# Expert stage of an audio tower: first weights stationary, bias folded into the gelu, token ids routed before the scores

## The reference

```python
h = tok(x)                                    # 16 x 255 tokens, 256 wide
h = h + attn(layernorm(h))                    # gated scan over the tokens, 8 heads
x = layernorm(h)                              # (16*255, 256)
logits = x @ w_red @ normalised(wg).T         # 8 experts
gates = softmax(logits); scores = max(gates); idx = argmax(gates)
g = gelu(x @ W1[idx] + b1[idx])               # 256 -> 512, exact gelu
o = (g @ W2[idx] + b2[idx]) * scores          # 512 -> 256
return h + o
```

## Time and profile before

| | us |
|---|---|
| median of 3 runs | 554.67 (554.56 to 558.87) |
| the profiled execution itself | 554.61 |
| its span in the trace | 552.9 |
| PE busy | 511.7 (93% of the span) |
| DVE, ACT, POOL busy | 454.5, 231.4, 193.1 |
| expert stage, first up product to last result | 412.8 to 543.0 |

### The profile page before, as it was taken

The page is one execution under the profiler, slowest core; times in us unless marked ns, Lnnn a source line. Parts: engine busy times, 40 slices in busy tenths (PEclk is TensorE's granted clock), DMA queues, the critical chain, the costliest instruction groups (busy, mean ns, idle before and its releaser), DMA issues. The chain is left out here.

```text
span 552.9 us, 12548 instructions
## 1 busy us (share of the span) xinstructions
PE 511.7 (93%) x3439; PEld 368.3 (67%) x3439; DVE 454.5 (82%) x1180; ACT 231.4 (42%) x447; POOL 193.1 (35%) x283
## 2 busy tenths in 40 slices
PE   5998999999999999999988879999868999999992
PEld 4875667766677766777654657777436777777771
DVE  2878888988889888888898899999858888888881
ACT  0436354664545554545635421222105444444440
POOL 5553323312232213222121212222142656665642
PEclk9999999999999999999998998999989999999997
DMA  5711212122122121221123033443521222222320
GB/s 126 249 40 38 76 40 76 43 71 76 38 76 67 47 76 47 67 76 38 38 54 97 24 99 98 114 107 92 209 96 41 85 73 86 74 81 79 78 56 1
DMA packets 34937, 42.14 MB, mean 76 GB/s; under 512 B 8454, under 2 KB 26103, under 8 KB 34644
## 3 DMA queue, kind: packets, MB, share of 16 engines
q1 hardware_dynamic: 25508, 27.59, 16.5%
q0 software_dynamic: 3744, 9.34, 5.8%
q10 hardware_dynamic: 5648, 4.75, 2.8%
HBM read 32.97 MB, written 9.59 MB: 77 GB/s over the span
## 5 line engine op out<-in xcount | busy, mean ns | idle before, releaser
L533 PE MATMUL banks<-proj,xnT_h 128*128 128x512 f16 x384 | 115.1, 382 | 4.3 <-DVE early L1231 4.2
L514 PE MATMUL banks<-early 128*128 128x256 f16 x768 | 86.8, 273 | 1.1 <-DVE early L1206 1.1
L514 PEld LDWEIGHTS banks<-early 128*128 128x128 f16 x768 | 75.1, 98 | 9.7 <-DVE early L1206 1.4
L533 PE MATMUL banks<-proj,xnT_l 128*128 128x512 f16 x192 | 73.1, 381 | 0.0
L533 PEld LDWEIGHTS banks<-proj,xnT_h 128*128 128x128 f16 x384 | 37.5, 98 | 41.2 <-DVE early L1231 4.9
L1855 POOL DMA_INDIRECT vo<-token_rows,vo x39 | 40.1, 1028 | 54.8 <-DVE proj L1689 35.3
L767 PE MATMUL banks<-w2h,vo 128*128 x312 | 57.5, 273 | 0.2 <-DVE vo L1664 0.2
L748 PE MATMUL banks<-w1h,vo 128*128 x156 | 52.9, 380 | 2.8 <-DVE vo L1657 2.8
L1003 ACT ACTIVATE vo<-banks 128x256 f16<-128x256 f32 x39 | 14.9, 383 | 81.0 <-PE banks L735 81.0
L1793 POOL TENSOR_TENSOR w1l<-stage,w1h 128x512 f32 (+1 forms) x16 | 19.0, 1186 | 84.0 <-ACT w1h L887 84.0
L1860 POOL DMA_INDIRECT out<-proj,vo x39 | 39.8, 1020 | 18.8 <-issue 10.8
(11 more groups left out here) (259 smaller groups left out, 1256.5 us busy)
## 6 DMA issues: line engine op xcount, KB each, us to landing
early<-in_x SPq DMA_DIRECT2D x16, 512.0 KB, 3.3
stage<-in_W SPq DMA_DIRECT2D x32, 256.0 KB, 2.8
early<-lam_by_chunk SPq DMA_DIRECT2D x32, 68.0 KB
token_rows<-rows ACTq DMA_DIRECT2D x16, 129.0 KB, 2.5
early<-lam_by_head SPq DMA_DIRECT2D x16, 128.0 KB, 3.0
rows<-in_b SPq DMA_DIRECT2D x1, 2048.0 KB, 7.1
token_rows<-rows ACTq DMA_DIRECT2D x16, 112.9 KB, 2.0
rows<-in_b SPq DMA_DIRECT2D x1, 1024.0 KB, 9.2
```

Of the source, the lines that this page charges most:

```text
L514: last = mm(bank(2 + j, D), x_[:, k, at:at + P], w[:, KG * half + k, :], start=(half == 0 and k == 0 and x_ is gT_h and w is wtok_h), stop ...
L533: last = mm(dst, a, c, start=(i == 0), stop=(i == n - 1))
```

## The change

What it does, part by part:

1. `up` swaps its operands: the weights are stationary and the rows stream. Per slot there are 4 (groups of 128 hidden units) x 2 x 3 = 24 matmuls of 128 columns where there were 6 of 512. The result has hidden units on the partitions, in two banks for each of two buffers, so it needs no turning: `transpose_gelu` is gone.
2. The bias of a unit is then one number per partition. ACT adds it inside the gelu, four ACTIVATEs of 128 columns per slot, with the bias's address from a register (ACT loads the expert number too). DVE's `add_bias` is gone. The bias table is a 16 KB load, turned once by PE; the 2 MB load is gone.
3. The split of the gelu reads SBUF; `down` runs one slot behind `up`, no longer two; `xh` and `xl` have two buffers.
4. The ids are found by their own product (32 matmuls of 39 columns), straight after the first `carried` table and `at_place`; the scores by a second one (32 of 78 columns) behind it. DVE makes `gather_id` ahead of the score halves, and the rest of the score work (`keep_scores`) after the first two slots' rows. POOL makes the arguments of the exponential.
5. `keep_busy(9)` after mixing tile 6, 30 for 28 in routing, 10 between the two find products, none behind them.

```diff
-            def up(i, e):
+            def up(i, v, e):
                 pe.wait_ge(s["xdl_done"], i + 1)
-                if i >= 1:
-                    pe.wait_ge(s["pre_done"], i)
-                for c in range(DC):
-                    for x_, w in ((xh, w1h), (xh, w1l), (xl, w1h)):
-                        last = mm(bank(0), x_[:, c, :], w[:, bass.ds(e * DC + c, 1), :].rearrange("p a b -> p (a b)"),
-                                  start=(c == 0 and w is w1h and x_ is xh), stop=(c == DC - 1 and x_ is xl))
-                last.then_inc(s["m1_ready"], 1)
-
-            def transpose_gelu(i, w):
-                pe.wait_ge(s["gelu_done"], i + 1)
                 if i >= 2:
-                    pe.wait_ge(s["g_done"], i - 1)
+                    pe.wait_ge(s["gelu_done"], FC * (i - 1))
                 for f in range(FC):
-                    last = tr(bank(4 + w)[:, f * P:f * P + P], gel[:, f * P:f * P + P], ident[:])
-                last.then_inc(s["gt_ready"], 1)
+                    for c in range(DC):
+                        for w, x_ in ((w1h, xh), (w1l, xh), (w1h, xl)):
+                            last = mm(banks[:, 4 * v + f // 2, f % 2 * P:f % 2 * P + P],
+                                      w[:, bass.ds(e * DC + c, 1), f * P:f * P + P].rearrange("p a b -> p (a b)"), x_[:, v, c, :],
+                                      start=(c == 0 and w is w1h and x_ is xh), stop=(c == DC - 1 and x_ is xl))
+                    if f % 2 == 1:
+                        last.then_inc(s["m1_ready"], 1)
...
             for i in range(SLOTS):
-                up(i, experts[i])
                 if i + 1 < SLOTS:
                     experts[i + 1] = expert_of(i + 1)
                     transpose_rows(i + 1)
+                up(i, i % 2, experts[i])
                 if i >= 1:
-                    transpose_gelu(i - 1, (i - 1) % 2)
-                if i >= 2:
-                    down(i - 2, i % 2, experts[i - 2])
...
+                    down(i - 1, (i - 1) % 2, experts[i - 1])
...
+            def gelu(i, w, e):
+                if i >= 2:
+                    act.wait_ge(s["g_done"], i - 1)
+                for f in range(FC):
+                    if f % 2 == 0:
+                        act.wait_ge(s["m1_ready"], 2 * i + f // 2 + 1)
+                    af(gel[:, w, f, :], banks[:, 4 * w + f // 2, f % 2 * P:f % 2 * P + P], ACT.Gelu,
+                       bias=b1_turned[:, bass.ds(e * FC + f, 1)]).then_inc(s["gelu_done"], 1)
...
+            pe.wait_ge(s["carried_ready"], 1)
+            find(found_ids, 0, 1).then_inc(s["found_ready"], 1)
+            keep_busy(10)
             pe.wait_ge(s["carried_ready"], 3)
...
+            find(banks[:, 7, 0:2 * SLOTS], 1, 2).then_inc(s["scores_found"], 1)
...
+                    if (p, k) == (1, 2):
+                        keep_busy(9)
```

More of the change, by code:

```diff
@@ L709, in _ @@
                 pair(p, ahead=p < PAIRS - 1)
+            pe.wait_ge(s["b1_in"], 16)
+            tr(bank(4, E * FC), b1_rows, ident[0:E * FC, 0:E * FC]).then_inc(s["b1_mm"], 1)
             keep_busy(14)
@@ L716, in _, with find @@
             mm(bank(0, 256), count_rows[:, 0, :], ohf, start=True, stop=True).then_inc(s["counts"], 1)
-            keep_busy(28)
-            pe.wait_ge(s["carried_ready"], 3)
[L721 to L728, removed]
+            keep_busy(30)
+            def find(dst, v, n):
+                for q in range(4):
+                    if n == 1:
+                        pe.wait_ge(s["places_ready"], q + 1)
+                    for t in range(8 * q, 8 * q + 8):
+                        last = mm(dst, at_place[:, t // 2, :, t % 2],
+                                  carried[:, t // 2, v:v + n, :, t % 2].rearrange("p v i -> p (v i)"),
+                                  start=(t == 0), stop=(t == TILES - 1))
+                return last
+            pe.wait_ge(s["carried_ready"], 1)
+            find(found_ids, 0, 1).then_inc(s["found_ready"], 1)
+            keep_busy(10)
+            pe.wait_ge(s["carried_ready"], 3)
+            find(banks[:, 7, 0:2 * SLOTS], 1, 2).then_inc(s["scores_found"], 1)
             def transpose_rows(i):
@@ L1603, in _ @@
                       slot_twice[:].unsqueeze(1).to_broadcast(TS), ALU.is_equal))
+            r.settle()
+            tt(carried[:, :, 0], in_slot, by_pairs(ids16[:]).unsqueeze(2).to_broadcast(TS),
+               ALU.mult).then_inc(s["carried_ready"], 1)
+            for q in range(4):
+                four = slice(4 * q, 4 * q + 4)
+                TP = [P, 4, P, 2]
+                tt(at_place[:, four], by_pairs(place_of)[:, four].unsqueeze(2).to_broadcast(TP),
+                   place_twice[:].unsqueeze(1).to_broadcast(TP), ALU.is_equal).then_inc(s["places_ready"], 1)
             dve.wait_ge(s["r_exp"], 1)
@@ L1611, in _ @@
             r.step(tt(score, score, valid[:], ALU.mult))
+            dve.wait_ge(s["found_ready"], 1)
+            ts(gather_id, found_ids, float(ID_MIDDLE), None, ALU.add).then_inc(s["route_ready"], 1)
             r.settle()
@@ L1619, in _ @@
                    ALU.mult).then_inc(s["carried_ready"], 1)
-            for q in range(4):
-                four = slice(4 * q, 4 * q + 4)
-                TP = [P, 4, P, 2]
-                tt(at_place[:, four], by_pairs(place_of)[:, four].unsqueeze(2).to_broadcast(TP),
-                   place_twice[:].unsqueeze(1).to_broadcast(TP), ALU.is_equal).then_inc(s["places_ready"], 1)
             S7 = [P, SLOTS, E - 1]
@@ L1631, in _, with keep_scores @@
             copy(sloti, slotf).then_inc(s["experts_ready"], 1)
-            dve.wait_ge(s["found_ready"], 1)
-            ts(gather_id, found[:, 0], float(ID_MIDDLE), None, ALU.add).then_inc(s["route_ready"], 1)
-            r.step(copy(score_high, found[:, 1]))
-            r.settle()
-            r.step(tt(slot_score, found[:, 2], score_high, ALU.add))
-            r.settle()
-            r.step(ts(empty, slot_score, 0.0, float(OUT_OF_RANGE + ID_MIDDLE), ALU.is_equal, ALU.mult))
-            r.step(ts(slot_id, found[:, 0], float(ID_MIDDLE), None, ALU.add))
-            r.settle()
-            r.end()
-            tt(store_id, slot_id, empty, ALU.add).then_inc(s["slot_ids_ready"], 1)
+            def keep_scores():
+                dve.wait_ge(s["scores_found"], 1)
+                r.step(copy(score_high, found_scores[:, 0]))
+                r.step(ts(slot_id, found_ids, float(ID_MIDDLE), None, ALU.add))
+                r.settle()
+                r.step(tt(slot_score, found_scores[:, 1], score_high, ALU.add))
+                r.settle()
+                r.step(ts(empty, slot_score, 0.0, float(OUT_OF_RANGE + ID_MIDDLE), ALU.is_equal, ALU.mult))
+                r.settle()
+                r.end()
+                tt(store_id, slot_id, empty, ALU.add).then_inc(s["slot_ids_ready"], 1)
             def norm_rows(i):
@@ L1850, in _ @@
                 root2(2 * h + 1)
+            T8 = [P, TILES, E]
+            pool.wait_ge(s["mx_done"], 1)
+            ptt(lg, rows[:, :, ROWC:ROWT], mx.unsqueeze(2).to_broadcast(T8), ALU.subtract).then_inc(s["lg_steps"], 1)
+            pool.wait_ge(s["rstd2_ready"], TILES)
+            pool.wait_ge(s["lg_steps"], 1)
+            ptt(lg, lg, rows[:, :, 1:2].to_broadcast(T8), ALU.mult).then_inc(s["r_args"], 1)
             def load(i):
```

116 lines of the change are left out of this document (52 added, 64 removed).

## The result

The changed kernel takes 581.06 us (median of 4 runs, 580.54 to 581.36) where the kernel before, run beside it, takes 555.12 (554.56 to 558.87). The ratio is 1.045, 95% interval 1.040 to 1.050: slower, by about 26 us. Its profiled execution took 580.99 us; the span is 579.2.

What follows compares the result with a forecast made beforehand. The prediction took the array to bound the kernel before (3.26 us a slot) and PE's queue after (3.97). 554.61 + 24.9 (expert stage) - 3.3 (routing) - 0.5 (keep_busy) = 575.7 us, range 570 to 582.

Steps and rivals of the forecast that it cites:

- The queue bounds the slot: Expert stage: after the change PE's instruction queue, not its array, sets the slot; forecast with its range, chance 0.79.
- The slot, 3.97: Steady expert stage: one slot takes 3.97 us by PE's queue, for 3.26 before; 36 such steps.
- The fill: Start of the expert stage: the third step begins 7.9 us after the first rows on DVE.
- C: Expert stage: PE's pauses halve the clock, 643 us, or 598 if in a third of slots; chance 0.06 with D.
- The tail: End of the expert stage: after the 36 steps end at 150.8, the last result begins at 156.7 us.
- Routing, -3.3: Routing: shorter work ahead of the gather starts the first rows 3.6 us earlier, taken as 3.3.
- The 0.3 against it: Routing: 0.3 us set against the earlier start, as the score product may delay the first rows' transposes.
- keep_busy(9), -0.5: Mixing stage: unread matmuls after tile 6 fill PE's pause and keep the clock; saves 0 to 1.4 us, taken as 0.5.
- The other engines: Expert stage: ACT (2.9 us), DVE and POOL (2.7 us) per slot none reach 3.97, so their savings give nothing.
- Rival A: Expert stage: register instructions cost nothing, the array stays the bound, slot 2.85 us, time 534; chance 0.11.
- B: Expert stage: only up is slow, value load and down hide, slot 3.50 us, time 559; chance 0.04.
- D: Expert stage: a step is longer with weight loads from a register, 0.33 us, time 601; chance 0.06 with C.

Runs made afterwards that it cites:

- the hoisted one: Changed kernel with byte offsets, four expert numbers per unchecked load, and up's and down's addresses computed ahead in five fused register instructions per slot: 536.44 us.
- addresses computed once: Changed kernel, but PE loads slot 0's expert number once and uses its weights for all slots, addresses staying in registers: 536.02 us.
- all constant: Changed kernel, but up and down read expert 0's weights at constant addresses and PE loads no expert number: 538.29 us.
- that kernel with the three edits: Kernel before with byte offsets, four expert numbers per unchecked load, and addresses computed at once ahead of the matmuls: 555.91 us, ratio 1.000.
- the first experiment: Changed kernel, but up always reads expert 0's weights at constant addresses; number load and down left as they are: 538.24 us.

## Why the prediction was right, point by point

The sign and the mechanism held: 575.7 forecast, 581.06 measured. By its steps:

- *The queue bounds the slot* (forecast 0.79). Shown three ways: spared register work gives 45 us to the changed kernel, none to the kernel before, and many short products make the kernel before slower than the changed one (593.83).
- *The slot, 3.97.* Measured 4.09 by the value loads, and (563.77 - 416.99) / 36 = 4.08 by the results: 36 x 0.11 = 3.9 us more than forecast. This is the term that was mis-sized. The usual step is the forecast's (in `up`, from 425 to 560, the 231 distances between the first register instructions of neighbouring triples have the median 0.242), but 52 of them are above 0.26, up to 0.41, and the mean is 0.256. One long step, 0.40 from the first `w1l` to the second, and a usual one behind it:

```profile
465.53 0.22 PE L760 MATMUL banks<-vo,w1l 128*128 128x128 f16 x1
...
465.93 0.22 PE L760 MATMUL banks<-vo,w1l 128*128 128x128 f16 x1
...
466.18 0.22 PE L760 MATMUL banks<-vo,w1l 128*128 128x128 f16 x1
```

  Seven steps within `up` at 0.256 and three within `down` at 0.259, for 0.246, make the 0.11. From load to `up` it is 0.90 on the mean (0.94 forecast); from `up` to `down` 0.37 and from `down` to the load 0.26, where the forecast has 0.35 and 0.25. The long steps were there to be read before: in the kernel before, the steps of `down` from 425 to 560 have the median 0.246 and the mean 0.263, and the places of the earlier trace rows hold none of the long ones. What makes a step long is open: a register instruction itself lasts 46 to 60 or 32 ns throughout.
- *The fill.* Forecast: the third step begins 7.9 us after the first rows. The first result came 9.6 after (407.37 to 416.99), 1.6 late. The clock is half there from 411 to 414, behind PE's pauses of 1.45 and 1.28 us; the prediction's C saw such spells as a risk of the steady stage, where none came in this kernel. It explains about half of the 1.6 by an estimate from other versions: in the array-bound ones the same distance is 8.7 with full clock (the hoisted one), 9.6 with 3.4 us of half clock (addresses computed once) and 10.2 with 6.8 (all constant). The rest is open.
- *The tail.* From the result of `down` 36 to the last forecast 5.8 (156.7 - 150.8, less 0.1 for DVE to begin), measured 568.86 - 563.77 = 5.1. With these the 161.5 us are whole: 156.7 + 1.6 + 3.9 - 0.7.
- *Routing, -3.3.* Measured -3.4. The 0.35 us from the two operations on POOL were in my 3.6 and did not come: DVE's scans, which wait for PE's counts, begin at 393.7 in both kernels. The 0.3 against it was not needed.
- *keep_busy(9), -0.5.* It does what it should: the clock is 1.00 from 328 to 336 and the wait of 0.71 is gone. The distance from DVE's addition for tile 6 to that for tile 7 is 2.66 us (333.20 to 335.86), for 3.43 in the kernel before (332.38 to 335.81) and 3.79 in that kernel with the three edits, which lacks the nine products too:

```profile
333.95 0.40 DVE L1537 TENSOR_TENSOR rows<-banks,rows 128x264 f32<-128x264 f32 x1
...
337.74 0.43 DVE L1537 TENSOR_TENSOR rows<-banks,rows 128x264 f32<-128x264 f32 x1 [1.06 <-PE banks L685]
```

  In the profiled execution both kernels still end mixing at 389.21, because this one was 0.8 us later at every tile up to tile 6 (333.20 for 332.38), from before the first of them, where the change touches nothing. So about 0.8 to 1.1, hidden here by the scatter of one execution.

- *The other engines* never came last, as forecast.
- *Rival A*, the array as the bound at 534, is not this kernel, but it is what the swap is worth once the queue is out of the way: 536. *B* assumed that the queue could run ahead in `down`. It can when its sum is below the array's, as the first experiment shows; in the changed kernel it is 1.1 to 1.2 us above. *C*: no spell of half clock came in this kernel's steady stage, but the argument against it was weak. It leaned on the eight matmuls of the earlier trace rows at full clock; the 22 behind them went 0.10 apart because the clock had fallen to half, from 403.8 to 407.2, behind the wait of 3.84. *D* (0.33 a step) did not occur as the rule; single steps reached 0.41.

```profile
403.80:404.40 0.60, 0.60 (x8) 0.60 (x8) 0.50 0.00 0
```

(L724 of the kernel before: PE, PEld, granted clock, DMA.)

Where my own reading fell short is in the expectations rather than the forecast: for the first experiment I added the array's time to the queue's, and missed by 17 us.

## What to carry to other kernels

Ask of every matmul that a change makes shorter what the engine's queue does between two of them. Sum the queue by itself and the array by itself, with prices from rows that average over many slots (two places that look alike can miss the longer steps), and take the larger; never add one's parts to the other's. Busy share does not show which it is; the distance of the starts does, together with "issue" as the only thing that the engine waits for.

If the queue is the bound, count instructions, not sums: compute a block's addresses at once ahead of it, fetch several indices with one load, and leave out range checks that an earlier step already guarantees. Then the shorter form can be worth what it promised.

## What the hardware showed that I had not expected

- A pair of weight load and matmul with an address that needs no arithmetic passes PE's queue in 0.04 us or less where the address is constant (32 pairs in 1.20 us). Where it waits in a register the pairs still keep up with the array's 0.055 (slots 2.83 and 2.83).
- Register arithmetic costs by the instruction: a fused one with, by the count above, six sums 74 ns, a single sum 32 ns. With what lies between them the two register instructions of a step make at least 0.242 - 3 x 0.04 = 0.12 us of it, an estimate from the usual step and the 0.04 of a pair.
- A load of four numbers into registers took 0.33 us, one of eight 1.95. The two also read different tiles, so whether it is the number or the place is open.
- Copies inside SBUF by DMA, 512 KB a slot of 2.9 us, raised the traffic from 88 to 271 GB/s beside gathers and stores, and the slot from 2.88 to 2.90.
- A quarter of the queue's steps is longer than the rest, 0.26 to 0.41 us for 0.24, in the changed kernel and in the kernel before. What holds them up is not shown.
- The granted clock fell to half, for 3 to 10 us, in the first slots of most of these kernels, behind two pauses of PE of 1.0 to 2.0 us with little work between them. In the hoisted version it stayed full behind pauses of 1.47 and 1.26, where the changed kernel had 1.45 and 1.28 and half clock. Such a pause goes before the spell and does not by itself bring it.
